# Two attention layers as one stream of slots in one block, with another order of work on each engine

## The reference, cut

```python
q = (x @ Wq.T).reshape(B, N, 12, 32)                       # third layer
k = (x @ Wk.T).reshape(B, N, 12, 32)
v = (x @ Wv.T + bv).reshape(B, N, 12, 32)
a = einsum('bnhd,bmhd->bhnm', q, k) * SCALE + encoding_bias # encoding_bias is adj
a = where(all(a == 0, axis=-1), -inf, a)
o = einsum('bhnm,bmhd->bnhd', nan_to_num(softmax(a)), v)
return o @ Wo.T + bo
...
q, k, v = heads(x @ Wq + bq), heads(x @ Wk + bk), heads(x @ Wv + bv)   # fourth layer
scores = q @ k.T / sqrt(32) + beta * adj
scores = where(adj > 0, scores, -9e15)
out = softmax(scores) @ v
```

## Time and profile before

| | |
|---|---|
| median of 3 runs | 3090.41 us (3089.36 to 3090.95) |
| the profiled execution | 3087.28 us |
| its span, first to last instruction | 3085.2 us |
| mean granted clock of TensorE | 0.98 |
| busy: TensorE, VectorE, GpSimd, ScalarE | 2926.5 (95%), 2301.9 (75%), 1375.3 (45%), 1155.7 us (37%) |

### The profile page before, as it was taken

How to read it: one execution, slowest core, us unless ns; L and a number is a source line. 1 busy time by engine, 2 the same in 40 slices (tenths; PEclk the granted TensorE clock), 3 DMA queues, 4 the chain that set the end, 5 groups by cost and what they waited for, 6 DMA issues and landing times. The chain is left out here.

```text
span 3085.2 us, 57599 instructions
## 1 busy us (share of the span) xinstructions
PE 2926.5 (95%) x22080; PEld 2491.0 (81%) x22080; DVE 2301.9 (75%) x5311; ACT 1155.7 (37%) x2369; POOL 1375.3 (45%) x1207
## 2 busy tenths in 40 slices
PE   8999999999599999999999599999999789999997
PEld 7988888889488888888887488888888677888886
DVE  6788888888557766766775688888888667777777
ACT  3344443444322222222222234434443234444443
POOL 6755576556465555555554232222222212332233
PEclk9999999999799999999999799999999999999998
DMA  5121121111211101100110111101111011111111
GB/s 141 31 68 47 50 62 58 61 47 54 87 54 49 39 25 35 49 29 25 45 49 11 55 51 45 45 23 45 45 33 36 34 37 45 46 45 46 56 45 44
DMA packets 134641, 145.98 MB, mean 47 GB/s; under 512 B 56800, under 2 KB 132320, under 8 KB 134368
## 3 DMA queue, kind: packets, MB, share of 16 engines
q1 hardware_dynamic: 134368, 142.31, 14.9%
HBM read 91.96 MB, written 50.33 MB: 46 GB/s over the span
## 5 line engine op out<-in xcount | busy, mean ns | idle before, releaser
L1908 POOL TENSOR_TENSOR l_prob<-l_prob,l_mx 128x512 f32<-128x512 f32 x192 | 200.7, 1045 | 774.9 <-DVE l_mx L1745 774.9
L1135 DVE TENSOR_TENSOR l_val<-l_ring,l_vec 64x384 f32<-64x384 f32 x512 | 284.6, 556 | 75.6 <-PE l_ring L950 68.7
L950 PE MATMUL l_ring<-whi,l_hhi 128*128 128x384 f32 x1152 | 272.8, 345 | 5.8 <-POOL wlo L79 5.8
L950 PE MATMUL l_ring<-wlo,l_hhi 128*128 128x384 f32 x1152 | 263.4, 336 | 0.0
L950 PE MATMUL l_ring<-whi,l_hlo 128*128 128x384 f32 x1152 | 263.3, 336 | 0.0
L1499 PE MATMUL l_ring<-l_hhi,whi 128*128 128x512 f32 x576 | 234.9, 408 | 9.5 <-DVE l_hlo L1725 9.2
L680 POOL TENSOR_TENSOR l_hlo<-l_hf,l_hhi 128x512 fp32r<-128x512 f32 x96 | 128.5, 1362 | 256.0 <-DVE l_hhi L477 256.0
L1499 PE MATMUL l_ring<-l_hlo,whi 128*128 128x512 f32 x576 | 228.8, 397 | 0.0
L1499 PE MATMUL l_ring<-l_hhi,wlo 128*128 128x512 f32 x576 | 228.8, 397 | 0.0
L445 ACT ACTIVATE l_mt<-l_ring 128x512 f32<-128x512 f32 x192 | 115.2, 600 | 292.0 <-PE l_ring L345 292.0
L950 PEld LDWEIGHTS l_ring<-whi,l_hhi 128*128 128x128 f32 x1152 | 200.7, 189 | 24.6 <-issue 18.6
(11 more groups left out here) (211 smaller groups left out, 7050.2 us busy)
## 6 DMA issues: line engine op xcount, KB each, us to landing
l_hf<-xt SPq DMA_DIRECT2D x16, 864.0 KB, 5.5
l_x<-x SPq DMA_DIRECT2D x16, 768.0 KB, 4.5
x<-l_za SPq DMA_DIRECT2D x16, 768.0 KB, 4.5
x<-l_zb SPq DMA_DIRECT2D x16, 768.0 KB, 3.6
l_xa<-x SPq DMA_DIRECT2D x16, 768.0 KB, 4.9
l_xb<-x SPq DMA_DIRECT2D x16, 768.0 KB, 6.5
x<-l_zfa SPq DMA_DIRECT2D x8, 768.0 KB, 3.5
x<-l_zfb SPq DMA_DIRECT2D x8, 768.0 KB, 4.3
```

The source lines that it names most:

```text
L950: mm = nc.tensor.matmul(ring[k % RING][:, 0:D], hh[:, c, first:first + P], ww[:, c, :], start=(j == 0), stop=(j == len(terms) - 1))
L1135: ins = nc.vector.tensor_tensor(val[half, (g + b) % GRAPHS, 0:D], ring[k % RING][half, 0:D], bias[half, :], ALU.add)
L1908: nc.gpsimd.tensor_tensor(row, row, mx[:, c, ts, :].rearrange("p t h -> p (t h)").unsqueeze(2) .broadcast_to([P, 2 * HP, S]), ALU.subtract)\
```

## The change

`heads_pass` is called once, with the inputs and outputs of both layers, and runs 32 slots in one block: 0 to 15 belong to the third layer, 16 to 31 to the fourth (`project(n)`). Buffers exist once. What each engine does in what order is new:

- `swap` and `sides` are gone. VectorE writes the values with their bias straight into `val`, two of four operations from one half of the partitions to the other.
- Queries and keys of slot n are computed in slot n itself, in the order query, key, query, key: queries always in `ring[0]`, keys in `ring[1]`. ScalarE copies all four heads of a key block; `keys_out` of VectorE is gone. The scores of a chunk follow one product after its keys.
- `output` alternates between the two graphs for each pair of heads; the last tile's output stands in the next slot, behind its first query product.
- Rows are turned into the score banks and `ring[1]`, late in the slot before. Turned outputs go to the `pt` and `ot` banks.
- The scaling of the last layer norm goes from VectorE to ScalarE (four operations, `final_apply`). The third layer's residual on GpSimd becomes four operations, and stands between the fourth and the fifth `take_off`.
- SyncE loads x and adjacency of slot n+1 in slot n; slots of the fourth layer first wait until the third layer's result of that group is stored.

The core of the diff, with the lines that are new or stay (those taken out stand in the functions above); it shows TensorE's query_key, the inner loops of output, TensorE's list, ScalarE's query_key and list, VectorE's values_out and list, GpSimd's list:

```diff
...
+            def query_key(n, k):
+                w, m = weight(n, k % 2), k // 2
+                if k >= 2:
+                    pe.wait_ge(qk_evac, 2 * KC * n + k - 1)
+                elif k == 1:
+                    pe.wait_ge(lo_done, KC * (n + 1))
+                else:
+                    pe.wait_ge(v_evac, max(T * n - 1, 0))
...
+                for m in range(PAIRS):
+                    for b in range(2):
+                        rows = slice(S * b, S * b + S)
...
+            for n in range(slots):
+                before = project(n - 1)
+                if n == groups:
+                    pe.wait_ge(sh.w_ready, 19)
+                query_key(n, 0)
+                if n:
+                    output(n - 1, 3)
+                query_key(n, 1)
+                if before:
+                    outputs_turned(n - 1, range(0, 2))
+                query_key(n, 2)
                 chunk_scores(n, 0)
+                query_key(n, 3)
+                if before:
+                    outputs_turned(n - 1, range(2, 4))
+                query_key(n, 4)
                 chunk_scores(n, 1)
+                query_key(n, 5)
+                pe.wait_ge(qk_evac, 2 * KC * n + 5)
+                if before:
+                    if n == 1:
+                        pe.wait_ge(sh.w_ready, 16)
+                    result(n - 1, 0)
+                    chunk_scores(n, 2)
+                    result(n - 1, 1)
+                    pe.wait_ge(w_evac, T * (n - 1) + 1)
+                    value(n, 0)
+                    pe.wait_ge(w_evac, T * (n - 1) + 2)
+                    result(n - 1, 2)
+                    pe.wait_ge(v_evac, T * n + 1)
+                    value(n, 1)
+                    pe.wait_ge(w_evac, T * (n - 1) + 3)
+                    result(n - 1, 3)
+                    probs_turned(n, 0)
+                    pe.wait_ge(v_evac, T * n + 2)
+                    value(n, 2)
+                    probs_turned(n, 1)
+                    output(n, 0)
+                    pe.wait_ge(w_evac, T * n)
+                    value(n, 3)
+                else:
+                    value(n, 0)
+                    chunk_scores(n, 2)
+                    value(n, 1)
+                    probs_turned(n, 0)
+                    pe.wait_ge(v_evac, T * n + 1)
+                    value(n, 2)
+                    probs_turned(n, 1)
+                    output(n, 0)
+                    pe.wait_ge(v_evac, T * n + 2)
+                    value(n, 3)
+                probs_turned(n, 2)
+                output(n, 1)
+                if n + 1 < slots:
+                    rows_turned(n + 1)
+                probs_turned(n, 3)
+                output(n, 2)
+            output(slots - 1, 3)
...
+            def query_key(n, k):
+                c = k // 2
+                act.wait_ge(qk_done, 2 * KC * n + k + 1)
+                act.wait_ge(s_done, max(KC * (n - 1) + c + 1, 0))
+                if k % 2 == 0:
+                    parts = [(slice(0, P), q[:, c, :], ring[0][:, :])]
+                else:
+                    parts = [(part, keys[part, c, :, h, :], ring[1][part, :].rearrange("p (g j) -> p g j", j=S))
+                             for h in range(HP) for part in [slice(HD * h, HD * h + HD)]]
+                for part, out, src in parts:
+                    if project(n):
+                        ins = nc.scalar.activation(out, src, ACT.Copy)
                     else:
+                        ins = nc.scalar.activation(out, src, ACT.Identity, bias=colvec[part, k % 2, c:c + 1])
+                ins.then_inc(qk_evac, 1)
...
+            for n in range(slots):
+                before = project(n - 1)
+                if n == groups:
+                    act.wait_ge(col_in, 16 * 3)
+                query_key(n, 0)
+                query_key(n, 1)
+                query_key(n, 2)
+                if before:
+                    outputs_high(n - 1, range(0, 2))
+                exponential(n, 0)
+                query_key(n, 3)
+                if before:
+                    outputs_high(n - 1, range(2, 4))
+                exponential(n, 1)
+                query_key(n, 4)
+                exponential(n, 2)
+                query_key(n, 5)
+                exponential(n, 3)
+                exponential(n, 4)
+                exponential(n, 5)
+                probs_out(n, 0)
+                probs_out(n, 1)
+                if n:
+                    final_apply(n - 1)
+                probs_out(n, 2)
+                if n + 1 < slots:
+                    high_parts(n + 1)
+                probs_out(n, 3)
+            final_apply(slots - 1)
...
+            def values_out(n, t):
+                bias = rowvec[:, 2 * (n // groups), :].rearrange("p (m q f) -> p m q f", q=2, f=HD)
+                bank = ring[t % 2 if not project(n - 1) else (0, 0, 0, 1)[t]]
+                dve.wait_ge(v_done, T * n + t + 1)
+                dve.wait_ge(o_done, max(T * (n - 1) + t + 1, 0))
+                src = bank[:, 0:D].rearrange("p (m q f) -> p m q f", q=2, f=HD)
+                for b in range(2):
+                    rows = slice(S * b, S * b + S)
+                    for p in range(2):
+                        ins = nc.vector.tensor_tensor(val[S * p:S * p + S, 2 * t + b, :, p, 0:HD], src[rows, :, p, :],
+                                                      bias[rows, :, p, :], ALU.add)
+                ins.then_inc(v_evac, 1)
...
+            for n in range(slots):
+                before = project(n - 1)
+                if n:
+                    divide(n - 1, 3)
+                maxima(n, 0)
+                maxima(n, 1)
+                if before:
+                    outputs_low(n - 1, range(0, 4))
                 split_weights(sh, dve, "hi", *weights_of_slot(n))
+                maxima(n, 2)
+                maxima(n, 3)
+                if n + 1 < slots:
+                    additive_mask(n + 1)
+                if n and not before:
+                    final_stats(n - 1)
+                maxima(n, 4)
+                if before:
+                    result_out(n - 1, 0)
+                maxima(n, 5)
+                if before:
+                    result_out(n - 1, 1)
+                    values_out(n, 0)
+                    result_out(n - 1, 2)
+                    values_out(n, 1)
+                    result_out(n - 1, 3)
+                    final_stats(n - 1)
+                    values_out(n, 2)
+                    final_shift(n - 1)
+                    divide(n, 0)
+                    values_out(n, 3)
+                else:
+                    if n:
+                        final_shift(n - 1)
+                    values_out(n, 0)
+                    values_out(n, 1)
+                    values_out(n, 2)
+                    divide(n, 0)
+                    values_out(n, 3)
+                divide(n, 1)
+                if n + 1 < slots:
+                    low_parts(n + 1)
+                divide(n, 2)
+            divide(slots - 1, 3)
+            final_stats(slots - 1)
+            final_shift(slots - 1)
...
+            for n in range(slots):
+                before = project(n - 1)
+                if n and not before:
+                    residual(n - 1, range(T - 1, T))
+                take_off(n, 0)
+                take_off(n, 1)
+                split_weights(sh, pool, "lo", *weights_of_slot(n))
+                take_off(n, 2)
+                take_off(n, 3)
+                if n and not before:
                     final_power(n - 1)
+                if project(n):
+                    residual(n, range(T))
+                take_off(n, 4)
+                take_off(n, 5)
+                if before:
+                    final_power(n - 1)
+                if not project(n):
+                    residual(n, range(T - 1))
+            residual(slots - 1, range(T - 1, T))
+            final_power(slots - 1)
...
```

More of the change, by code:

```diff
@@ L1406, in heads_pass @@
         fpow_done = sem("fpow_done")
+        fb_done = sem("fb_done")
         y_done = sem("y_done")
         dve_steps = sem("dve_steps")
-        final_steps = sem("final_steps")
-        mask_steps = None if project else sem("mask_steps")
         block = ctx.enter_context(nc.Block())
-        def slots(eng, body):
-            def turn(i, last):
-                for a in range(2):
-                    body(2 * i + a, i, a, isinstance(i, int) and i == 0 and a == 0, last and a == 1)
-            in_turns(eng, iters, turn)
@@ new lines, in _ @@
+            load_x(0)
+            load_adj(0)
+            for k in range(3):
+                sync.dma_start(rowvec[:, k, :], rowvec_d[k]).then_inc(vec_in, 16)
+            load_x(1)
+            load_adj(1)
+            for k in range(2):
+                sync.dma_start(colvec[:, k, :], colvec_d[k], allow_slow_non_contiguous=True).then_inc(col_in, 16)
+            sync.dma_start(beta[:, :], beta_d).then_inc(col_in, 16)
+            load_weights(sh, sync, 15, 19)
+            for n in range(slots):
```

(45 more changed lines are left out.)

578 lines of the change are left out of this document (185 added, 393 removed).

## The result

The changed kernel takes 3159.98 us (median of 4 runs, 3156.73 to 3165.11) against 3090.43 us, a ratio of 1.0229 with a 95% interval of [1.0215, 1.0242]. It is 70 us slower; 3140 was forecast, with 3100 to 3200 as the range. The profiled execution took 3158.62 us, its span is 3156.8 us.

What follows compares the result with a forecast made beforehand. TensorE was taken as the bound; 3.5 to 4 us saved per slot would be more than given back as waits. Slots add about +32 and +54 us, the change of layers -36: 50 us more, 3140 us, range 3100 to 3200.

Steps and rivals of the forecast that it cites:

- Prices: Costs of TensorE's steps from the earlier trace: nine value products 1.66 us, eight scores 1.88, a tile's outputs 1.37.
- part 2: Outputs on TensorE alternating array halves: 0.78 us a tile in place of 1.37, 2.4 us less a slot.
- rival of outputs that stay at 57 ns: TensorE's outputs gain nothing from alternating: 77 us more, 3217 us; chance 0.08.
- Part 1: Exchange products leave TensorE: some 1.2 us and a 0.5 us wait a slot; VectorE's crossing writes cost nothing extra.
- Part 3: ScalarE copies four key heads serially, 2.76 us (fourth layer) or 2.38 (third); TensorE waits 1.01 us in the fourth.
- rival of overlapping head copies: ScalarE's head copies overlap; if four took the time of two, 96 us go: 3044 us; chance 0.11.
- Part 4: ScalarE's exponential ahead of the next key block: chain between scores 8.23 us (fourth layer), 8.38 (third); TensorE waits 1.55 to 2.74.
- Part 5: Slot's tail from the third scores: 15.82 us (fourth layer), 22.26 (third); slots become 40.37 and 46.85 us.
- Part 6: Final scaling on ScalarE (2.2 us a slot), GpSimd's residual and VectorE's mask and statistics all stay hidden.
- Part 7: One stream removes clearing, first load and drain at the change of layers: 36 us less.
- rival of a stream that does not join: Something holds the fourth layer's first slot, so the 36 us come back: 3176 us; chance 0.07.
- the rival that the prediction held at one in ten: TensorE's clock falls in the new waits: 1.74 us an episode, 31 make 54 us, 3194 us; chance 0.10.

Runs made afterwards that it cites:

- e2: The changed kernel with the outputs back in the old order, all pairs of one graph and then of the other; 3224.52 us, ratio 1.0446.
- b1: The kernel before with only the exchange removed: VectorE writes odd heads' values straight into the other half of the partitions; 3082.66 us, ratio 0.9984.
- e1: The changed kernel with ScalarE's key block of the second and third chunk moved ahead of the previous chunk's exponential; 3072.14 us, ratio 0.9953.
- e8: The changed kernel with nine unread products ahead of the third scores and also of the fourth layer's transposes of probabilities; 3137.45 us, ratio 1.0156.
- e4: The changed kernel with key blocks shared again, two heads copied by ScalarE and two by VectorE between the maxima; 3118.95 us, ratio 1.0105.

## Why the prediction was right, point by point

**Prices and part 2 (outputs).** 24 outputs were priced at 0.78 us by the second layer's pattern; the distance of starts is 0.86 (36 ns each, not 31), so a tile gains 0.51 us and not 0.6. e2 bears out 2.1 us in a slot against the 2.4 forecast. The rival of outputs that stay at 57 ns is out.

**Part 1 (values across halves).** The price of crossing was right: 16 such operations in a fourth-layer slot take 355 ns on average, against 347 in the earlier trace rows, two of four of them crossing. By their place in the loop the two that cross take 351 and 360 ns, the two that stay 347 and 361. They don't overlap, as the prediction had it: four take 1.46 us and not 1.3. The Trainium skill (Vector Engine (DVE) Microarchitecture Reference, 3.8 The reshape front-end and per-opcode configuration) lets an operation on 33 to 64 partitions write to either half; it says free of cost only of 32-partition moves, and the trace shows the same of 64. What was wrong is the worth of the step taken alone: 5 us in b1 and not the 1.7 us a slot that the prediction gives it, 1.4 in a fourth-layer slot and 0.9 lost in a third-layer one, where by the rows VectorE is next. In the changed kernel this doesn't show, as its slots wait for ScalarE.

**Part 3 (keys by ScalarE alone).** Four heads take 2.74 us (2.76 forecast), end to end. The rival of overlapping head copies (3044 us, the one on the faster side) is out by that row. The uncovered 1.01 us of a block stands in e1's 7.10 us between scores.

**Part 4 (ScalarE's order).** The step that decides held. The chain is 7.96 us against 8.23 in the fourth layer and 8.18 against 8.38 in the third: ScalarE begins the copies as the exponential ends with an overlap of 0.1 us (2708.53 against 2708.64), and the scores follow 0.06 us behind the copies, where 0.15 was allowed. e1 undoes this step alone: 85 us, more than all that the change lost; some 69 of them are the chain.

**Part 5 and the slots.** 40.13 us against 40.37, 46.57 against 46.85, the mixed slot 45.08 against 45.75. The shorter chains are partly taken up by outputs at 0.86 us.

**Part 6 (hidden moves).** ScalarE's scaling takes 2.50 us and not 2.2 and stays hidden. The mask's tensor_scalar takes 1.15 us beside GpSimd's subtraction (0.28 for its neighbour without one) and costs nothing, as VectorE then waits for scores anyway; these are the rows of that slot's groups:

```profile
L1725 DVE TENSOR_SCALAR h_on<-h_adjpa,h_beta 128x256 f32<-128x256 f32 x1 | 1.2, 1153 | 0.0
...
L1724 DVE TENSOR_SCALAR h_off<-h_adjpa 128x256 f32<-128x256 f32 x1 | 0.3, 283 | 0.0
```

What part 6 did not look at is the weight split, which also stands between subtractions in one slot. The third scores of that slot start 20.13 us after its first, not 16.37: 3.8 us.

**Part 7 (one stream).** 37.3 us went at the change of layers, 36 were forecast. The rival of a stream that does not join is out.

**The sum.** The forecast span was 3135.7 us; 3156.8 was measured, 21.1 more. By the slots' own lengths: the low clock adds 25 (10.4 in fourth-layer slots, 10.6 in the third's from slot 2 on, about 4 in slots 0 and 1, an estimate by what is left there), the weight split 3.8, and the shorter chains take 8.4 back; 0.7 lie at the ends. So the rival that the prediction held at one in ten was half true: its price for an episode was 1.74 us, and an episode costs 1.65, but there are fewer, six of fourteen full slots of the fourth layer and ten of fourteen of the third, there often a part of one, and the rival stood as an alternative to the forecast when it should have been a term of it. The rows that it was priced from the earlier trace rows are a little more mixed than the prediction says: in the last slot twelve transposes and a second wait of 0.96 us stand between the idle 2.52 us and the slow outputs. Filled (e8), the span is 3133.5 us, 2.2 under the forecast; that it is so near is partly luck, as the weight split and the shorter chains, 3.8 and 8.4 us, have opposite signs. The prediction listed a low clock within slots as a sign against itself, and it was one: the chain that decides was right, and the term that the sum put at nothing is the low clock, 25 us of the 70.

## What to carry to other kernels

A list that an engine works through in order is part of the dependences: a copy that is ready but stands behind an operation whose input takes a detour over two other engines inherits that detour. Read for each wait of the bounding engine what its releaser did between the arrival of the input and the release (here 0.9 us of waiting for another engine's result and of its exponential), and change the places of the two before sharing out the work. And price each part of a rewrite alone against the old order: here the two cheap edits to TensorE's list gave 2.1% without the rewrite, one of them only in the layer where the engine behind it had room.

## What the runs showed of the hardware that was not expected

- TensorE's low clock came behind waits of 1.6 to 2.4 us that recur in each slot, but in the changed kernel's fourth layer only in every second slot, with the same products and the same wait in the slot between. In e4, where the wait is 4.1 us on average, it came in every full one. Filling one wait with 1.66 us of products that nobody reads moved it to the next wait of 1.6 us, filling both took it away, and the mean granted clock over the span rose from 0.976 to 0.981 and 0.988. Only these fillers were tried; which of their properties counts was not.
- A GpSimd subtraction can hold up very small VectorE operations. Two of 4 and 12 columns took 2.34 and 2.30 us beside 2.6 us subtractions of 1152 columns. The Trainium skill (SBUF — State Buffer, SBUF: two separate sides) calls the port pair of both an exclusive lock that is held for the whole instruction, and these rows agree. It does not hold up all: the maxima beside the same split in the changed kernel took no longer than elsewhere. Where a long GpSimd operation is moved to therefore depends on what VectorE does beside it.
